# A state-space block on one core: readout sums in two PSUM banks and ahead of the inputs, B turned in the first stage, pieces of u turned in steps, last stores in eight parts

## The reference, cut to what matters

```
x = x + 0.5 * ffn(layernorm(x))                       # 256 -> 1024 -> gelu -> 256
x = x + ssm(layernorm(x))
x = x + 0.5 * ffn(layernorm(x))

ssm:  xb, gate = split(rmsnorm(x) @ W_in.T)           # 512 channels each
      xc = silu(causal_conv4(xb))
      dt = soft_clamp(softplus(xc @ W_dt.T + b_dt));  Bp = xc @ W_B.T;  Cp = xc @ W_C.T    # 16 states
      for every t:  h = h * exp(soft_clamp(dt * A)) + dt * Bp * xc     # 512 x 16 states a sequence
                    if t % 10 == 0:  h = h * min(20 / norm(h), 1)
                    y = sum over n of h * Cp, + D * xc
      out = x + scale * ((y * silu(gate)) @ W_out.T)
```

## Time and profile before

| | us |
|---|---|
| median of 3 runs | 1645.36 (1644.27 to 1646.35) |
| the profiled execution | 1644.98 |
| its span, first to last instruction | 1643.1 |
| PE busy | 1461.6 (89%) |
| PEld busy | 986.7 (60%) |
| DVE busy | 1278.2 (78%) |
| ACT busy | 1112.3 (68%) |
| POOL busy | 986.4 (60%) |

### The profile page before, as it was taken

The page is one execution under the profiler, slowest core; times in us unless marked ns, Lnnn a source line. Parts: engine busy times, 40 slices in busy tenths (PEclk is TensorE's granted clock), DMA queues, the critical chain, the costliest instruction groups (busy, mean ns, idle before and its releaser), DMA issues. The chain is left out here.

```text
span 1643.1 us, 24197 instructions
## 1 busy us (share of the span) xinstructions
PE 1461.6 (89%) x6460; PEld 986.7 (60%) x6460; DVE 1278.2 (78%) x2555; ACT 1112.3 (68%) x2515; POOL 986.4 (60%) x1350
## 2 busy tenths in 40 slices
PE   6999999999688888888888888888888888999998
PEld 5555555554456566656665656665665665677776
DVE  7657656655578888888887888887888889877885
ACT  4355445557978888888887888887888874243333
POOL 1202222012479898989988889898998999700000
PEclk9999999999789999999999999999999999999999
DMA  7222355125565555656655565555655436465430
GB/s 251 77 79 91 117 146 143 66 92 189 164 182 158 162 152 140 172 149 168 160 154 151 137 174 133 158 161 141 178 153 155 135 98 198 122 208 171 137 116 26
DMA packets 232654, 236.84 MB, mean 144 GB/s; under 512 B 46120, under 2 KB 198376, under 8 KB 232520
## 3 DMA queue, kind: packets, MB, share of 16 engines
q1 hardware_dynamic: 231576, 233.99, 49.7%
q10 hardware_dynamic: 944, 1.31, 0.2%
HBM read 136.84 MB, written 98.68 MB: 143 GB/s over the span
## 5 line engine op out<-in xcount | busy, mean ns | idle before, releaser
L1145 DVE TENSOR_TENSOR_SCAN h<-decay,banks 128x352 f32<-128x352 f32 x820 | 710.5, 882 | 56.8 <-POOL hc L948 1.5
L948 POOL TENSOR_TENSOR hc<-h,bc 128x320 f32<-128x320 f32 x820 | 655.1, 821 | 30.6 <-PE banks L995 28.4
L995 PE MATMUL banks<-hc,w_ident 128*128 128x320 f32 (+1 forms) x1664 | 543.6, 452 | 47.6 <-ACT yc L1084 38.6
L1050 ACT ACTIVATE tb<-dtc,a 128x320 f32<-128x320 f32 (+1 forms) x832 | 416.3, 554 | 4.8 <-DVE x L562 4.8
L995 PEld LDWEIGHTS banks<-hc,w_ident 128*128 128x128 f32 x1664 | 291.8, 196 | 125.5 <-POOL hc L948 39.8
L1072 ACT ACTIVATE decay<-tb 128x640 f32<-128x640 f32 x410 | 296.3, 723 | 0.4
L938 POOL TENSOR_TENSOR rc<-qs,w_mhalf 128x1 f32<-128x1 f32 x410 | 225.9, 551 | 114.9 <-DVE qs L1129 106.0
L983 PE MATMUL banks<-ub 128*128 128x176 f32 x1640 | 283.9, 297 | 10.9 <-DMA ub<-scratch_ub 10.9
L976 PEld LDWEIGHTS banks<-sc_ss,sc_ones 128*128 128x128 f32 x820 | 134.6, 197 | 263.8 <-ACT sc_sq L1061 246.2
L1061 ACT ACTIVATE sc_sq<-h 128x64 f32<-128x64 f32 x410 | 128.1, 313 | 189.1 <-issue 100.0
L983 PEld LDWEIGHTS banks<-ub 128*128 128x128 f32 x1640 | 227.4, 201 | 12.2 <-DMA ub<-scratch_ub 11.2
(11 more groups left out here) (117 smaller groups left out, 1562.1 us busy)
## 6 DMA issues: line engine op xcount, KB each, us to landing
ub<-scratch_ub SPq DMA_DIRECT2D x410, 107.5 KB
bc<-scratch_blk SPq DMA_DIRECT2D x205, 160.0 KB, 3.6
scratch_ub<-turned SPq DMA_DIRECT2D x64, 512.0 KB, 4.1
scratch_ub<-spread SPq DMA_DIRECT2D x64, 176.0 KB, 4.3
scratch_xc<-xc SPq DMA_DIRECT2D x8, 1024.0 KB, 4.8
scratch_sg<-sg SPq DMA_DIRECT2D x8, 1024.0 KB, 5.9
scratch_dt<-dt SPq DMA_DIRECT2D x8, 1024.0 KB, 5.9
scratch_u<-u SPq DMA_DIRECT2D x8, 1024.0 KB, 6.7
```

The lines of the kernel that those rows point to most:

```text
L948: pool.tensor_tensor(hc[:, pl % 2, x * kh * B * N:(x + 1) * kh * B * N, j % QB * S:(j % QB + 1) * S] .rearrange("p (c b n) e -> p c b n e" ...
L995: mm = pe.matmul(psY[:, 0:KE * B * wide], w.ident[:], rhs, start=(n == 0), stop=(n == N - 1))
L1050: act.activation(tanh_rows(c, r), dtc[:, c % 2, k * B:(k + 1) * B, 0:blocks_of(c) * S].rearrange("p b (k e) -> p k b e", e=S), ACT.Tanh, s ...
L1145: dve.tensor_tensor_scan(state(m).rearrange("p r e -> p (r e)")[:, half], decay[:, m % DRING, half], psI[m % B][:, half], 0.0, ALU.mult, A ...
```

## The change

1. **Readout.** The sums of even groups go to bank 2, those of odd ones to bank 5 (up to group 48), so a readout waits for the copy of the group two back (`y_before`). In TensorE's step the readout chunk stands before the inputs instead of behind them. `copy_y` moves by one unit.
2. **B.** B isn't part of a piece any more. After `project_bc` and the projection of x, TensorE turns B of a whole tile (`turn_b`, a new entry "bt" of the ring), ScalarE copies it (`copy_bt`), GpSimd cuts it into two parts and spreads it in four products into two buffers (`spread_b`), and SP stores these (`store_b`). In the first stage, `spread_b(i-1)` is the last thing in GpSimd's tile i, and `store_b(i-2)` stands in SP's tile i behind `store_bc(i-1)`. B of tile 6 is stored behind `load_units`, B of tile 7 within the scan: products at units 8, 12, 16, 20, stores at blocks 6, 8, 10, 12. `masks` moves from tile 4 to tile 0.
3. **Pieces of u** are made one every 10 units: four transposes in four steps, ScalarE's copy in two halves in the two units after, the vector engine's subtraction in the unit after those.
4. **dt and u of the last tile** are stored in eight transfers, one a block at blocks 1 to 8.

The diff, cut to what this text speaks of:

```diff
@@ -120,11 +120,13 @@
         if i >= 1:
             order.append(("bc", i - 1, 0))
         order += [("x", i, m) for m in range(KE)]
+        if i >= 1:
+            order.append(("bt", i - 1, 0))
         if 1 <= i < LAST:
             order += [("up", i + 1, m) for m in range(KH)]
         order += [("gate", i, m) for m in range(KE)]
         order += [("dt", i, m) for m in range(KE)]
-    order.append(("bc", TILES - 1, 0))
+    order += [("bc", TILES - 1, 0), ("bt", TILES - 1, 0)]
     use = {what: n for n, what in enumerate(order)}
     CONV = KE * TAPS
 
...
         store(sp, "u", u[:], u_out, i)
+
+    def store_last(sp, k):
+
+        name, tile, ready, done = ("dt", dt, dt_ready, dt_out) if k < KE else ("u", u, u_ready, u_out)
+        c = k % KE
+        sp.wait_ge(ready, LAST + 1)
+        sp.dma_start(dram[name][:, c * B:(c + 1) * B, steps(LAST)],
+                     tile[:, c, :].rearrange("p (b t) -> p b t", b=B)).then_inc(done, 16)
+
+    def stored(i):
+
+        return 16 * (i + 1) if i < LAST else 16 * (LAST + KE)
 
     def dt_u(dve, i):
         dve.wait_ge(th_ready, i + 1)
...
             if i in (6, 7):
                 scan.load_piece(sp, i - 5)
                 scan.store_piece(sp, i - 6)
+            if i >= 2:
+                scan.store_b(sp, i - 2, 0, G)
...
             else:
                 scan.load_units(sp)
+                scan.store_b(sp, LAST - 1, 0, G)
             if i == 3:
...
                 rstd1(i + 2)
             if i + 1 < TILES:
                 norm2(i + 1)
-            if i in (6, 7):
-                scan.mask_piece(pool, i - 6)
+            if i >= 1:
+                scan.spread_b(pool, i - 1, 0, G)
 
     def tensor(pe, scan):
...
@@ -344,6 +361,13 @@
             for k in range(KE):
                 mm = pe.matmul(out[0:2 * N, :], wbc[:, k, :], xc[:, i % 2, k, :],
                                start=(k == 0), stop=(k == KE - 1))
+            mm.then_inc(ring_done, 1)
+
+        def turn_b(i):
+            out = fill(("bt", i, 0))
+            pe.wait_ge(ring_read, use["bc", i, 0] + 1)
+            for q in range(G):
+                mm = pe.transpose(out[:, q * N:(q + 1) * N], bcs[0:N, q * P:(q + 1) * P], w.ident[0:N, 0:N])
             mm.then_inc(ring_done, 1)
 
         pe.wait_ge(consts, 1)
...
             project(i, "x", 0)
+            if i >= 1:
+                turn_b(i - 1)
...
                 act.wait_ge(ring_read, use["bc", i, 0])
             if i >= 1:
                 act.wait_ge(bc_out, 16 * i)
+                act.wait_ge(ring_done, use["bt", i - 1, 0] + 1)
             act.activation(bcs[:], src[0:2 * N, :], ACT.Copy).then_inc(ring_read, 1)
+
+        def copy_bt(i):
+            src = held(("bt", i, 0))
+            if i == LAST:
+                act.wait_ge(ring_read, use["bt", i, 0])
+            scan.copy_bt(act, i, src[:, 0:G * N], ring_read)
 
         act.dma_start(xt[:, 0, 2:4, :], dram["x"][1, steps(0), :].rearrange("(h p) d -> p h d", p=P)
...
+                scan.masks(dve)
             if i == 4:
                 scan.decay_scale(dve)
-                scan.masks(dve)
                 post.residual_steps(dve)
 
-    return Pre(sync, gpsimd, tensor, scalar, vector, dt_u, store_dt_u, order, use,
+    return Pre(sync, gpsimd, tensor, scalar, vector, dt_u, store_last, stored, order, use,
...
 
 def piece_unit(k):
 
-    return 12 * (k - B) + 2
+    return 10 * (k - B)
+
+
+def y_bank(p):
+
+
+    return 2 if p % B == 0 and p <= LAST_EVEN else 5
+
+
+def y_before(p):
+
+    return p - 2 if p <= LAST_EVEN + 1 else p - 1
 
 
...
@@ -790,7 +847,10 @@
 
     def load_unit(sp, m):
         j, b = m // B, m % B
-        sp.wait_ge(ub_out, 64 * (B * (min((j + 1) * S, L - 1) // P) + b + 1))
+        t = min((j + 1) * S, L - 1)
+        sp.wait_ge(ut_out, 32 * (B * (t // P) + b + 1))
+        for q in range(2):
+            sp.wait_ge(b_out[q], 2 * 16 * (G // 2) * (t // TT + 1))
         if m >= URING:
             sp.wait_ge(inp_ready, m - URING + 1)
...
-    def turn_piece(pe, k, out):
-        pe.wait_ge(piece_in, 32 * (k + 1))
-        if k >= 1:
-            pe.wait_ge(ut_lo, k)
-        for c in range(KE):
-            pe.transpose(out[:, c * P:(c + 1) * P], piece[:, c, :], w.ident[:])
-        pe.transpose(out[:, E:E + 2 * N], piece_b[:], w.ident[0:2 * N, 0:2 * N]).then_inc(ut_done, 1)
-
-    def high_piece(act, k, src):
-        act.wait_ge(ut_done, k + 1)
-        if k >= 1:
-            act.wait_ge(ub_out, 64 * k)
-            act.wait_ge(spread_done, k)
-        act.activation(turned[:, 0, :], src[:, 0:E + N], ACT.Copy).then_inc(ut_hi, 1)
+
+    def turn_piece(pe, k, out, c0, c1):
+        if c0 == 0:
+            pe.wait_ge(piece_in, 16 * (k + 1))
+            if k >= 1:
+                pe.wait_ge(ut_lo, k)
+        for c in range(c0, c1):
+            mm = pe.transpose(out[:, c * P:(c + 1) * P], piece[:, c, :], w.ident[:])
+        if c1 == KE:
+            mm.then_inc(ut_done, 1)
+
+    def high_piece(act, k, src, e0, e1):
+        if e0 == 0:
+            act.wait_ge(ut_done, k + 1)
+            if k >= 1:
+                act.wait_ge(ut_out, 32 * k)
+        act.activation(turned[:, 0, e0:e1], src[:, e0:e1], ACT.Copy).then_inc(ut_hi, 1)
 
     def low_piece(dve, k, src):
-        dve.wait_ge(ut_hi, k + 1)
-        dve.tensor_tensor(turned[:, 1, :], src[:, 0:E + N], turned[:, 0, :].bitcast(F32), ALU.subtract).then_inc(ut_lo, 1)
-
-    def mask_piece(pool, k):
-        pool.wait_ge(ut_lo, k + 1)
-        if k == 0:
-            pool.wait_ge(mask_steps, 2 + 2 * (S // 2))
-        if k >= 1:
-            pool.wait_ge(ub_out, 64 * k)
-        pool.tensor_tensor(
-            spread[:], turned[:, :, E:].bitcast(F32).unsqueeze(3).broadcast_to([P, 2, N, W]),
-            mask[:, k // B % (S // 2)].unsqueeze(1).unsqueeze(1).broadcast_to([P, 2, N, W]),
-            ALU.mult).then_inc(spread_done, 1)
+
+        dve.wait_ge(ut_hi, k + 1 if k < B else 2 * (k + 1) - B)
+        dve.tensor_tensor(turned[:, 1, :], src, turned[:, 0, :].bitcast(F32), ALU.subtract).then_inc(ut_lo, 1)
 
     def store_piece(sp, k):
         t, b = k // B * P, k % B
-        rows = dram["ub"][b, t:t + P].rearrange("t (r h) x -> t r h x", h=2)
         sp.wait_ge(ut_lo, k + 1)
         for r in range(2):
-            sp.dma_start(rows[:, r, :, 0:E], turned[:, :, 0:E].bitcast(F32)).then_inc(ub_out, 16)
-        sp.wait_ge(spread_done, k + 1)
-        for half in range(2):
-            sp.dma_start(rows[:, :, half, E:], spread[:].bitcast(F32).rearrange("p r n e -> p r (n e)")
-                         ).then_inc(ub_out, 16)
+            sp.dma_start(dram["ub"][b, t:t + P, 2 * r:2 * r + 2, 0:E], turned[:].bitcast(F32)).then_inc(ut_out, 16)
+
+
+
+    def copy_bt(act, i, src, read):
+        if i >= 1:
+            act.wait_ge(b_split, 2 * i)
+        act.activation(bt[:].rearrange("p q n -> p (q n)"), src, ACT.Copy).then_inc(read, 1)
+
+    def spread_b(pool, i, q0, q1):
+        if q0 == 0:
+            pool.wait_ge(pre.ring_read, pre.turn_of["bt", i, 0] + 1)
+            if i >= 1:
+                pool.wait_ge(spread_done, G * i)
+            pool.tensor_copy(bts[:, 0], bt[:]).then_inc(b_split, 1)
+            pool.wait_ge(b_split, 2 * i + 1)
+            pool.tensor_tensor(bts[:, 1], bt[:], bts[:, 0].bitcast(F32), ALU.subtract).then_inc(b_split, 1)
+            pool.wait_ge(b_split, 2 * i + 2)
+            if i == 0:
+                pool.wait_ge(mask_steps, 2 + 2 * (S // 2))
+        for q in range(q0, q1):
+            if G * i + q >= 2:
+                pool.wait_ge(b_out[q % 2], 2 * 16 * ((G * i + q) // 2))
+            pool.tensor_tensor(
+                spread[:, q % 2], bts[:, :, q].bitcast(F32).unsqueeze(3).broadcast_to([P, 2, N, W]),
+                mask[:, (i * TT // P + q % 2) % (S // 2)].unsqueeze(1).unsqueeze(1).broadcast_to([P, 2, N, W]),
+                ALU.mult).then_inc(spread_done, 1)
+
+    def store_b(sp, i, q0, q1):
+        for q in range(q0, q1):
+            t = i * TT + q % 2 * P
+            sp.wait_ge(spread_done, G * i + q + 1)
+            for half in range(2):
+                sp.dma_start(
+                    dram["ub"][q // 2, t:t + P].rearrange("t (r h) x -> t r h x", h=2)[:, :, half, E:],
+                    spread[:, q % 2].bitcast(F32).rearrange("p r n e -> p r (n e)")).then_inc(b_out[q % 2], 16)
 
     def masks(dve):
...
@@ -899,17 +979,19 @@
             if dk == 1 and dc + 2 < DCHUNKS:
                 sp.wait_ge(tanh_done, (dc + 1) * NCH)
                 load_dt(sp, dc + 2)
-            if j == 4:
-                pre.store_dt_u(sp, TILES - 1)
+            if 1 <= j <= 2 * KE:
+                pre.store_last(sp, j - 1)
+            if j in (6, 8, 10, 12):
+                store_b(sp, TILES - 1, j // 2 - 3, j // 2 - 2)
             if k == 1 and c + 2 < CHUNKS:
                 relayout(sp, c + 2)
+            if j - 4 in after:
+                store_piece(sp, after[j - 4])
```

(43 more changed lines are left out.)

46 lines of the change are left out of this document (25 added, 21 removed).

## The result

The changed kernel takes **1711.99 us** (median of 4 runs, 1711.26 to 1714.38) against 1645.86 of the kernel before on the same chip: ratio 1.0404, 95% interval 1.0386 to 1.0422. It is 66 us slower; 1702 was forecast. The kernel before was timed again beside the experiments and took 1649.60 to 1650.65 us there, so a difference between the times here and those of the experiments holds to about 5 us. The profiled execution has a span of 1709.8 us, 66.7 more than before.

A forecast was written before the change was run, and what follows sets the result against it. First stage: TensorE, busy 333 of 344 us; scan: the vector engine at 2.13 us a unit plus stalls. 1644.98 + 41.4 (hand-shake) + 6 (low clock) + 1 (hand-over) + 8 (scan) = 1702 us, range 1650 to 1730.

The forecast's parts named there:

- The hand-shake: First stage: GpSimd's third product waits for SP's stores, delaying the rsqrt queued behind it in tiles 2 to 5; 41.4 us slower.
- the low clock: First stage: TensorE runs slow after each such hole, 1.5 us in each of four tiles; 6 us (0 to 10).
- The turn of B: First stage: four added TensorE transposes a tile fit the hole of 0.60 us before the gate projection; nothing.
- rivals 1 to 3: Inputs not late, 1622 us (10%); inputs late but GpSimd's wait free, 1653 (11%); neither, 1574 (5%).
- The hand-over: First stage to scan: stores of B and GpSimd's late `ones` delay the first carry; 1 us, 0 to 4.
- The scan: Stalls at readout groups vanish, but late inputs and small disturbances spend the gain; +8 us (-6 to +24).
- The loop of total, readout, inputs, carry and scan: Scan: inputs behind the readout close a loop over two units, 4.81 us, 2.405 per unit; -5.2 us over 383 gaps.
- the small terms on top: Scan: pieces +7, GpSimd's last products +2, low clock +1.5, tanhs +2.5, first gaps -1.5, last steps +2 us.
- Both stalls at the readout groups go: Scan: two banks end TensorE's 1.05 us wait, the earlier readout end GpSimd's 0.69 us wait.
- Rival 1: Scan: inputs are not late, the vector engine stays the bound at 2.13 us a unit; 71 us less, 1622 us; 10%.
- two kinds of stalls: Scan before the change: waits at a readout group's end (GpSimd 0.69, TensorE 1.05 us) and at a piece of u (0.61 us).
- Rival 4, the low clock in the scan: TensorE's lower share drops the scan to the low clock, 3.3 us per unit; 2050 us if throughout; 2%.

The follow-up runs named there:

- e2: The changed kernel with GpSimd's third and fourth product of B moved behind the next tile's rsqrt: 1671.96 us, ratio 1.0134.
- e12: e7 with inputs behind the readout in each group's last step, and GpSimd's last two products of B after the tile's SiLU: 1603.65 us.
- e3: The changed kernel with both edits, inputs ahead of the readout and the last two products behind the rsqrt: 1606.07 us, ratio 0.973.
- e7: e3 with all four products of B and the two split operations behind the rsqrt: 1605.31 us, ratio 0.9728.
- e1: The changed kernel with the inputs of a step ahead of the readout chunk again: 1648.32 us, ratio 0.9993.
- e9: e6 with ScalarE's copy of the sums one unit earlier, where the kernel before has it: 1612.06 us, ratio 0.9769.
- e8: e3 with the last tile's eight stores of dt and u issued together in block 4 instead of one a block: 1609.97 us, ratio 0.9754.
- e11: e7 with a whole piece of u turned and copied in one step and subtracted in the next: 1649.18 us, ratio 0.9998.
- e4: The kernel before, still with one bank, with the readout chunk ahead of the inputs: 1794.37 us, ratio 1.086.
- e6: e3 with one bank for the readout sums instead of two: 1804.31 us, ratio 1.0919.
- e5: e3 with a group's readout cut unevenly, 3, 2, 2, 2, 2, 2, 2, 1 pairs of matmuls: 1599.82 us, ratio 0.9711.

## Why the prediction was right, and where it was not

**The hand-shake: mechanism and sum right, the sum by some luck.** Forecast were 41.4 and 6 for the low clock; the five tiles are 8.3, 8.5, 22.1, 7.8 and 0.7 us longer, 47.5. Inside, two sizes were off and cancel. In tile 3 the rsqrt comes 8.7 us late and not 9.4, the gate projection 6.1 and not 6.9: the fourth store landed 3.2 us after its issue and not 4.1. And the low clock behind the hole costs 2.4 us there (9.56 against 7.13) and not 1.5; over tiles 2 to 5 it is 10 us (9.78, 9.56, 9.41 and 9.92 us for the sixteen matmuls) and not 6. The row at low clock that was used was of shorter work. The hole of 0.60 grew to 6.19 only, since TensorE enters it 0.5 us later, by the turn of B. The Trainium skill, "TensorE: Matmul & The Clock Gate", section "HAM oscillation — how this bites in real kernels", has such a wait lower the clock anew in every tile; the trace agrees (9.41 to 9.92 us in each of the four tiles, against 7.13). That the wait is the cause e2 shows, by 40 us.

**The turn of B at nothing: right**, by e12, whose tiles are 49.70 with the turn in them. What no step named is that GpSimd's new products slow the vector engine where they overlap with the convolution: 1.1 us in tiles 2 and 3 of e2, e3 and e7. In the changed kernel itself the wait keeps them apart (0.747 us an operation, 0.744 before), so the sum didn't need it, but its rivals 1 to 3 did. The Trainium skill, "SBUF — State Buffer", section "🔬 SBUF: two separate sides", says that GpSimd and a vector operation with two inputs from SBUF lock a shared pair of ports against each other; e7 and e12 agree with it (5.16 us beside the products, 4.06 without), though no run shows that it is the ports.

**The hand-over: 1 forecast, 1.4 measured**, within its 0 to 4: from the last `norm2` to the first carry it is 53.6 us, where it was 52.2. The other 1.0 of the 49.9 lies ahead of these five tiles. GpSimd waits 16.67 us for a store of tile 6 and sets the ones at 475.09 (after).

**The scan: direction and loop right, disturbances undersized.** Forecast +8, measured +18.5. The loop of total, readout, inputs, carry and scan was put at 4.81 a pair and is 4.84: over 383 gaps 6 us. The middle gaps (units 9 to 392) sum to 944.2 us, and 934 were forecast (921.1 and 13). The remaining 4 are in the small terms on top, 17 where 13 were forecast; which of them is not told apart.

**The rivals were priced too low.** The sum stands, but of the sentence "Both stalls at the readout groups go" the rivals made more than it holds. In the changed order they do go (GpSimd's wait 28.4 to 11.6, TensorE's 38.6 to 0.6). With the inputs in front GpSimd's stays, 38.0 us in 49 groups of e1, since GpSimd (0.55 + 1.59 in a step of 2.13) is as full as the vector engine, which the prediction didn't reckon. Rival 1 gave 71 us off the middle of the scan; e1 shows 45 (926.3 to 881.0).

And the gain that is there has another source than it was put down to. Two parts were tried alone on e3: the second bank, together with the later copy, is worth 6 us (e9), spreading the stores 4 (e8). Where the 45 us of e1 lie can be read from its gaps between carries and those of the kernel before:

- The 29 gaps with a piece in them fall from 3.53 to 2.98 us on the mean: 16 us. GpSimd's product of 0.80, which leaves the scan too, costs nothing by itself: in the kernel before, the carries around it lie 2.13 us apart.

```profile
561.28 0.33 DVE L1135 TENSOR_SCALAR banks<-h,rc 128x64 f32<-128x64 f32 x1
561.45 0.80 POOL L855 TENSOR_TENSOR spread<-turned,mask 128x352 fp32r<-128x352 f32 x1
...
563.41 0.33 DVE L1135 TENSOR_SCALAR banks<-h,rc 128x64 f32<-128x64 f32 x1
```

- The largest part is one that the prediction overlooked when it named two kinds of stalls. In 13 of 47 readout groups of the kernel before, TensorE falls to the lower clock for 3 to 4 us: the granted clock of such a group is 0.91 or 0.92, of the others 1.00; these stretches are about half of what the 0.96 of the earlier trace rows lacks. In twelve of the 13 it falls behind two short waits with one step between them: for squares, shortly after a piece, and for the copy. Here is one, with the window of the low clock (0.59):

```profile
708.79 0.38 PE L976 MATMUL banks<-sc_ss,sc_ones 128*128 128x1 f32 x2 [1.02 <-ACT sc_sq L1061]
709.03 0.66 PE L983 MATMUL banks<-ub 128*128 128x176 f32 x4
710.75 2.42 PE L995 MATMUL banks<-hc,w_ident 128*128 128x320 f32 x4 [1.06 <-ACT yc L1084]
```

```profile
710.30:714.50 4.20, 3.75 (x11) 2.92 (x12) 2.21 (x6) 2.19 (x7) 2.29 (x4) 0.59 0.17 49
```

  Besides its pieces such a group takes 2.5 us more than eight times 2.13, a group of e1 0.8, and e1 has none at the low clock: 22 us.
- 3.5 us lie before unit 16, where the late load was, and 4 in the other 34 groups.

Which part of the change clears the low clock no run tries alone. It is hardly the bank: e9 has one bank and the copy where the kernel before has it, and two such groups instead of 13. What is left is the pieces in steps and without B (in e11, with whole pieces and two banks, there are three). So the scan adds up: 998.1, 46 off for all of this (951.9 in e1), and 64.7 for the order: 1016.6.

**Rival 4, the low clock in the scan**, had 2% and a price of 3.3 us a unit. It did not come here: none of the changed kernel's 47 groups is at the low clock. e4 and e6 are it in part, with 2.8 us a unit and a granted clock of 0.93 and 0.87 in the scan. Why the changed kernel is spared was not tried apart; e4, the same order on the kernel before, lacks the second bank and the pieces in steps both.

Still open: why in e5, and in the kernel before, some groups fall to the low clock and others with the same two waits don't (three of 15 in the kernel before), and what the remaining 0.28 us in one tile of e12 is. Its last tile, 50.13 us, is shorter than before (50.46).

## What to carry to other kernels

An in-order queue makes an added wait cost what stands behind it, so for each wait list the next instructions of that engine and their slack: 4.6 us of waiting for a store, and the work behind it, became 8.5 us in tile 3, because a rsqrt with 1.7 us of slack was queued behind; 2.4 of them are the low clock that followed. When an engine's work is swapped in a recurrence, add up the loop (0.54 + 2.01 + 0.06 + 2.20 gave the measured time within 1%) before counting the stalls that vanish. And judge a change by its parts: this one is 66 us slower, holds some 40 us of gain, and moving `inputs` and the last two products of a tile sets it free. A mean clock of 0.96 in a stage is worth following up before a forecast: here about half of what it lacked lay in 13 places, worth 22 us, that no list of busy times shows.

## What the runs showed that was not expected

- TensorE's clock fell to the lower level behind waits of 4.06 to 10.08 us, which was known from the earlier trace rows. But it fell too behind two short waits with one short step between them: 1.00 and 0.65 us in e5, 1.02 and 1.06 in the kernel before. Shortening one step can then give back what it won, as in e5.
- A copy that stands one unit later in ScalarE's queue costs 192 us with one bank (1804.31 against 1612.06); with two banks and the later copy TensorE waits 0.6 us for it in the whole scan (e1). Two banks with the earlier copy were not run.
- Two engines that overlap can slow each other without any wait in the profile: 4.06 against 5.16 us and 1.57 against 2.56. It shows only in the durations.
